# Dilated attention in a four-image transformer block: the sums over the taps move from VectorE to GpSimd

## The reference

```python
x = x + _L0_conv_ref(_ln_c(x), ...)        # halo attention
t = t + _L0_ffn_ref(_ln_t(t), ...)         # top-k routed feed-forward
x = x + _L1_conv_ref(_ln_c(x), ...)        # dilated attention, here is the change
t = t + _L1_ffn_ref(_ln_t(t), ...)         # graph attention routes a mixture of four experts

def _dilate_attention(q, k_, v, kernel, dil, head_dim):
    kw = _unfold_windows(k_, kernel, dil)   # nine shifted copies ("taps")
    vw = _unfold_windows(v, kernel, dil)
    attn = softmax(einsum('bndhw,bndkhw->bnkhw', qh, kw) * scale, axis=2)
    out = einsum('bnkhw,bndkhw->bndhw', attn, vw)      # the sum over nine taps
```

## Time and profile before

| what | value |
|---|---|
| median of 3 runs | 7053.45 us (7039.84 to 7058.35) |
| the profiled execution's own time | 7049.08 us |
| its span | 7047.3 us |
| mean granted TensorE clock | 0.693 of full speed |
| VectorE busy | 3414.0 us, 48% |
| TensorE busy | 2995.6 us, 43% |
| GpSimd busy | 2605.7 us, 37% |

### The profile page before, as it was taken

The page is one execution under the profiler, slowest core; times in us unless marked ns, Lnnn a source line. Parts: engine busy times, 40 slices in busy tenths (PEclk is TensorE's granted clock), DMA queues, the critical chain, the costliest instruction groups (busy, mean ns, idle before and its releaser), DMA issues.

```text
span 7047.3 us, 83154 instructions
## 1 busy us (share of the span) xinstructions
PE 2995.6 (43%) x31245; PEld 1791.3 (25%) x31245; DVE 3414.0 (48%) x7000; ACT 1543.3 (22%) x3959; POOL 2605.7 (37%) x2472
## 2 busy tenths in 40 slices
PE   0011149766987897788760222222222222222204
PEld 0011138424842673376220000000000000000103
DVE  9999988576857685777661111111111111111138
ACT  0000027403730463165200111111111111111100
POOL 0000000051011000100017777777777777777450
PEclk9975569866986798698755656565655555555556
DMA  2000040002000100010022222222122222222216
GB/s 82 0 0 0 0 168 4 4 18 56 4 12 1 40 3 1 13 17 3 1 33 22 34 33 33 33 33 33 28 31 33 33 29 31 33 33 33 65 46 218
DMA packets 259879, 227.73 MB, mean 32 GB/s; under 512 B 115180, under 2 KB 223128, under 8 KB 250456
## 3 DMA queue, kind: packets, MB, share of 16 engines
q0 software_dynamic: 78944, 29.28, 6.6%
q1 hardware_dynamic: 99960, 99.91, 4.6%
q10 hardware_dynamic: 80640, 93.86, 4.3%
HBM read 100.42 MB, written 121.39 MB: 31 GB/s over the span
## 4 chain that ended last, share of the span: by engine, by line
PE 27%; issue 20%; another core or an unknown queue 19%; DVE 19%; DVEq 7%; ACT 4%; DMA 3%; POOL 1%; ACTq 1%; SPq 0%
DVE SA_ L1325 3%; PE PSB L382 2%; PE PSB L1175 2%; DVE SA_ L1315 2%; PE PSB L686 2%; PE PSB L668 2%; PE PSB L352 2%; PE PSB L526 2%; DVEq L1406 2%; PE PSB L392 1%; PE PSB L518 1%; DVE SA_ L590 1%; DMA VPAD<-s_TNT 1%; PE PSB L366 1%
## 5 line engine op out<-in xcount | busy, mean ns | idle before, releaser
L962 POOL DMA_INDIRECT SA_<-s_T,GIX x2048 | 2166.4, 1058 | 675.7 <-issue 675.7
L1175 PE MATMUL PSB<-VPAD,EH 128*128 128x512 f32 x512 | 302.0, 754 | 1994.1 <-DMA VPAD<-s_TNT 1643.1
L907 DVE TENSOR_TENSOR XPAD<-SA_ 128x256 f32<-128x256 f32 x32 | 13.6, 425 | 1789.9 <-DMA SA_<-s_T,GIX 1789.9
L954 POOL DMA_INDIRECT s_AEXP<-fill,SIX x128 | 149.6, 1169 | 1557.3 <-DVE SA_ L587 1472.2
L858 POOL DMA_INDIRECT SA_<-s_SK,BLKI x128 | 131.5, 1028 | 1484.3 <-PE PSB L710 1389.0
L1175 PEld LDWEIGHTS PSB<-VPAD,EH 128*128 128x128 f32 x512 | 121.6, 246 | 2195.3 <-DMA VPAD<-s_TNT 1681.4
L1179 PE MATMUL PSB<-SA_,EW 128*128 128x512 f32 x512 | 345.6, 824 | 342.1 <-ACT SA_ L1160 181.0
L1429 PE MATMUL PSB<-ident,SA_ 128*128 128x128 f32 x448 | 83.1, 368 | 837.1 <-DVE SA_ L1396 575.1
L303 ACT ACTIVATE PRX<-PSB,MX 128x144 f32<-128x144 f32 x1024 | 375.2, 380 | 210.3 <-DVE MX L224 210.1
L1164 ACT ACTIVATE VPAD<-PSB,PRX 128x512 f32<-128x512 f32 x128 | 87.9, 687 | 1308.8 <-remote 969.0
L1160 ACT ACTIVATE SA_<-PSB,PRX 128x512 f32<-128x512 f32 x256 | 175.9, 687 | 770.6 <-issue 327.0
(11 more groups left out here) (365 smaller groups left out, 7339.3 us busy)
## 6 DMA issues: line engine op xcount, KB each, us to landing
SA_<-s_T,GIX POOLq DMA_INDIRECT x2048
s_Y<-VPAD ACTq DMA_DIRECT2D x32, 1024.0 KB
s_R<-zero SPq DMA_DIRECT2D x96, 256.0 KB, 2.9
s_R<-XPAD ACTq DMA_DIRECT2D x32, 768.0 KB
SB_<-s_Y SPq DMA_DIRECT2D x16, 1024.0 KB, 5.5
SA_<-s_Y SPq DMA_DIRECT2D x16, 1024.0 KB, 6.2
s_AEXP<-zero SPq DMA_DIRECT2D x32, 256.0 KB, 3.0
SA_<-in_x SPq DMA_DIRECT2D x16, 512.0 KB
```

The costliest lines, as they stand in the source:

```text
L962: pool.indirect_dma_start(out=n.G[:,s,c,:],out_offset=None,in_=d["T"],in_offset=IOA(ap=n.GIX[s][:,c:c+1],axis=0)).then_inc(n.gath[s],16)
L1175: pe.matmul(PSB[:,(m%4)*512:(m%4+1)*512],n.WM1[:,m//2,(m%2)*P:(m%2+1)*P],n.TNC[:,s,:],start=True,stop=True).then_inc(n.moe_h,1)
```

## The change

GpSimd does the additions over the taps. `value(m,j)` on VectorE keeps the multiplication alone. Its product goes to one of four buffers in turn: the two old ones, `REST`, and a piece of `SA`. Before it writes a buffer again it waits, on the new semaphore `s_ad`, for the addition four back. A new function `l1conv_pool` runs on GpSimd: for each unit and each tap j = 1 to 8 it waits for the product (`s_p2`), adds it to `ACC`, raises `s_ad`, possibly issues one indirect transfer, and drains. TensorE's `project` waits for `s_ad` in place of `s_acc`.

GpSimd's transfers are placed anew. Of the 128 block fetches, 48 are issued during image 0's feed-forward, 20 as keys and values are formed, and 60 behind the additions of image 0, one behind each. The 32 key fetches are unchanged. The scatters of images 1 to 3 come behind every second addition. The waits for `fill_done` and `np_rdy` stand before image 1's additions.

```diff
-    n.PRD=pr[:,0:6,:]; n.PR2=pr[:,6:8,:]; n.ACC=...
+    n.PRD=pr[:,0:6,:]; n.PR2=[pr[:,6,:],pr[:,7,:],n.REST[:,:],SA[:,19968:20480]]; n.ACC=...
@@ l1conv_dve
     def value(m,j):
         dve.wait_ge(n.s_ep,b*72+(9*m+j+1))
-        acc=n.ACC[:,m//2%2,m%2,:]; to=n.PR2[:,j%2,:] if j else acc
+        to=n.PR2[(j-1)%4] if j else n.ACC[:,m//2%2,m%2,:]
+        if j and 8*m+j>4: dve.wait_ge(n.s_ad,b*64+(8*m+j-4))
         bank=(9*m+j)%EBANKS
         dve.tensor_tensor(rows(to),rows(PSB[...]),tap(n.VD,m,TAPS[j]),ALU.mult).then_inc(n.s_p2,1)
-        if j:
-            dve.drain()
-            last=dve.tensor_tensor(acc,acc,to,ALU.add)
-            if j==8: last.then_inc(n.s_acc,1)
@@ l1conv_pe, project
-        if h==0: pe.wait_ge(n.s_acc,b*8+(2*u+2)); ...
+        if h==0: pe.wait_ge(n.s_ad,b*64+8*(2*u+2)); ...
@@ GpSimd
+HELD=48; PROJ=20
 def pos_pool(pool,m,n,d):
     pool.wait_ge(m.blk_rdy,1); pool.wait_ge(m.sk_st,16)
-    for t in range(NT):
-        if t<20: pool.wait_ge(n.s_kv,t+1)
-        else: pool.wait_ge(n.s_p2,(t-20)*66//108+1)
+    for t in range(HELD+PROJ):
+        if t<HELD: pool.wait_ge(n.s_h,t*2//3+1)
+        else: pool.wait_ge(n.s_kv,t-HELD+1)
+        block_pool(pool,m,n,d,t)
+def l1conv_pool(pool,m,n,d,b):
+    if b: pool.wait_ge(n.ad_ld,16*b)
+    for u in range(UNITS):
+        acc=n.ACC[:,u//2%2,u%2,:]
+        for j in range(1,9):
+            k=8*u+(j-1)
+            pool.wait_ge(n.s_p2,b*72+(9*u+j+1))
+            pool.tensor_tensor(acc,acc,n.PR2[(j-1)%4],ALU.add).then_inc(n.s_ad,1)
+            if b==0 and HELD+PROJ+k<NT: block_pool(pool,m,n,d,HELD+PROJ+k)
+            if b and j%2==0: start_pool(pool,n,d,(b-1)*TILES+k//2)
+            pool.drain()
@@ GpSimd's program
             pos_pool(pool,m,n,d)
+            l1conv_pool(pool,m,n,d,0)
+            keys_pool(pool,m,n,d)
+            pool.wait_ge(m.fill_done,FILLS); pool.wait_ge(n.np_rdy,1)
+            for b in range(1,IMGS): l1conv_pool(pool,m,n,d,b)
             V=blocks(pool,m)
-            pool.wait_ge(m.fill_done,FILLS)
             edges_pool(pool,n,d,m.tick,V)
```

More of the change, by code:

```diff
@@ L57, in declare_dense @@
     pr=SA[:,12288:16384].rearrange("p (k q) -> p k q",k=8)
-    n.PRD=pr[:,0:6,:]; n.PR2=pr[:,6:8,:]; n.ACC=SA[:,17408:19456].rearrange("p (u i q) -> p u i q",u=2,i=2)
+    n.PRD=pr[:,0:6,:]; n.PR2=[pr[:,6,:],pr[:,7,:],n.REST[:,:],SA[:,19968:20480]]; n.ACC=SA[:,17408:19456].rearrange("p (u i q) -> p u i q",u=2,i=2)
     n.LMX=sb("LMX",[P,4,8])
@@ L70, in declare_dense @@
     n.s_gt, n.s_tb, n.x3_st, n.tn_st, n.t_st, n.sorted_ = [sem(s) for s in ("s_gt", "s_tb", "x3_st", "tn_st", "t_st", "sorted_",)]
-    n.s_acc, n.s_ltc, n.s_lt, n.s_res = [sem(s) for s in ("s_acc", "s_ltc", "s_lt", "s_res",)]
+    n.s_ad, n.s_ltc, n.s_lt, n.s_res = [sem(s) for s in ("s_ad", "s_ltc", "s_lt", "s_res",)]
     n.s_ka, n.s_kd, n.s_p, n.s_pe, n.s_c0, n.s_r, n.s_c1, n.s_z = [sem(s) for s in ("s_ka", "s_kd", "s_p", "s_pe", "s_c0", "s_r", "s_c1", "s_z",)]
@@ L693, in project @@
         bank=pbank(u,h)
-        if h==0: pe.wait_ge(n.s_acc,b*8+(2*u+2)); pe.wait_ge(n.s_cqc,b*8+min(2*u+5,8))
+        if h==0: pe.wait_ge(n.s_ad,b*64+8*(2*u+2)); pe.wait_ge(n.s_cqc,b*8+min(2*u+5,8))
         if h==1 and u<3: pe.wait_ge(n.s_res,b*8+(2*u+1))
@@ L850, in pos_dve, with block_pool, keys_pool @@
     dve.drain()
+HELD=48; PROJ=20
+def block_pool(pool,m,n,d,t):
+    pool.indirect_dma_start(out=m.SI[:,t*BLK:(t+1)*BLK],out_offset=None,in_=d["SK"],in_offset=IOA(ap=m.BLKI[:,t:t+1],axis=0)).then_inc(n.gb_ld,16)
 def pos_pool(pool,m,n,d):
-    I=m.SI
     pool.wait_ge(m.blk_rdy,1); pool.wait_ge(m.sk_st,16)
-    for t in range(NT):
-        if t<20: pool.wait_ge(n.s_kv,t+1)
-        else: pool.wait_ge(n.s_p2,(t-20)*66//108+1)
-        pool.indirect_dma_start(out=I[:,t*BLK:(t+1)*BLK],out_offset=None,in_=d["SK"],in_offset=IOA(ap=m.BLKI[:,t:t+1],axis=0)).then_inc(n.gb_ld,16)
+    for t in range(HELD+PROJ):
+        if t<HELD: pool.wait_ge(n.s_h,t*2//3+1)
+        else: pool.wait_ge(n.s_kv,t-HELD+1)
+        block_pool(pool,m,n,d,t)
+def keys_pool(pool,m,n,d):
     pool.wait_ge(n.end_rdy,1)
@@ L862, in pos_pool, with start_pool @@
         if t>=4: pool.wait_ge(n.s_h,32+t-3)
-        pool.indirect_dma_start(out=I[:,t*128:(t+1)*128],out_offset=None,in_=rows,in_offset=IOA(ap=m.QI[:,t:t+1],axis=0)).then_inc(n.a2_ld,16)
+        pool.indirect_dma_start(out=m.SI[:,t*128:(t+1)*128],out_offset=None,in_=rows,in_offset=IOA(ap=m.QI[:,t:t+1],axis=0)).then_inc(n.a2_ld,16)
+def start_pool(pool,n,d,t):
+    pool.indirect_dma_start(out=d["AEXP"],out_offset=IOA(ap=n.SIX[:,t:t+1],axis=0),in_=n.ADN[:,t,:],in_offset=None,bounds_check=4096*128-1,oob_is_err=False).then_inc(n.ad_sc,16)
+def l1conv_pool(pool,m,n,d,b):
[9 more added lines that the diff above has]
+            pool.drain()
 def edges_prep_dve(dve,n,SA,V,ones,K,row):
@@ L945, in edges_pool @@
 def edges_pool(pool,n,d,tick,V):
[L947 to L954, removed]
+    pool.wait_ge(n.ad_ld2,16)
+    for t in range((IMGS-1)*TILES,NT): start_pool(pool,n,d,t)
     pool.wait_ge(n.d0_rdy,1)
```

## The result

| | before | after |
|---|---|---|
| median | 7048.5 us (7039.8 to 7058.4, 4 runs) | 7106.7 us (7106.0 to 7109.8, 4 runs) |
| span of the profiled execution | 7047.3 us | 7107.9 us |
| ratio | | 1.0083, 95% interval 1.0065 to 1.0100 |

The account below looks back on a forecast made before the run. The prediction took the bound to be a chain changing hands between VectorE and TensorE, neither full. Its terms summed to -81 + 30 + 22 + 8 = -21 us on 7049.1, giving 7028, stated as 7030; eight-in-ten range 6985 to 7085.

Parts of the forecast that it names:

- A transfer step: GpSimd's indirect fetch or scatter behind an addition: 0.94 us plus a 0.30 us gap, 1.25 us in all.
- rival 3: GpSimd becomes the bound, at image 0's buffer waits and all tails: 7060 us, near 7100 beyond the upper end; chance 0.20.
- The price of one addition: One addition on GpSimd: 1.15 us, middle of 0.69 and 1.57, plus a 0.30 us gap, 1.45 a step.
- Term 4: Image 0's units, where GpSimd's work nearly fills the unit: 2 us less gain in each of four units, 8 us.
- Term 3: Each image's tail, unit 7, where the projection waits for the slower GpSimd additions: 5.5 us lost an image, 22 in all.
- term 1: Additions leaving VectorE's chain in the four images: 26 x 0.78 = 20.3 us gained an image, 81 in all.
- term 2: GpSimd additions delaying VectorE's products and scaling at the same SBUF: 7.6 us lost an image, 30 in all.
- rival 2: Products and scaling wait in full for GpSimd additions: 14 us an image, 56 in all, total near 7050; chance 0.20.
- It just fits: Buffer wait within a unit: fourth addition ends about 2157.9 us, before the last multiplication is due at 2158.2, so no cost.
- Rival 1: GpSimd and VectorE do not disturb each other at SBUF, that cost is zero: total 6998 us; chance 0.18.
- Edits at nothing: 48 fetches moved to image 0's feed-forward, the moved waits and TensorE's clock were all counted as costing nothing.
- What would show it: Signs listed for right or wrong, such as additions of about 1.15 us and four stages together about 986 us, from 1007.

Follow-up runs that it names:

- the quarter additions: Changed kernel with each GpSimd addition covering only 128 of 512 columns, the other sums left out; 6990.0 us, 0.9929 of the kernel before.
- the fills: Changed kernel with each GpSimd addition replaced by a memset of 1024 columns of an unused tile, sums left out; 7030.5 us, 0.9978 of the kernel before.

## Why the prediction was wrong

The step that failed is "A transfer step is 0.94 + 0.30 = 1.25". I had read the 0.30 off two fetches in a row, with no drain behind either. With the drain a fetch costs 3.97 - 1.43 = 2.54 us and a scatter 5.16 - 2 x 1.43 = 2.30, twice as much. Image 0's unit was to hold 21.6 us of GpSimd and holds 31.8. That is the mechanism of rival 3, at its place, the wait on `s_ad` in image 0 and the tails. But I had tied it to an addition of 1.57 us or more and gave image 0's unit 25 us even then. The addition was not what was wrong.

Image 0's units were to be 20.3 - 7.6 - 8 = 4.7 us shorter and are 43.9 longer. These 49 us, 14 more in image 0's tail, 10.5 in the feed-forward, which I had put at nothing, and 8.5 in the tails of images 1 to 3 are the miss of about 80 us.

Point by point:

- *The price of one addition.* Forecast 1.15 + 0.30 = 1.45 a step, measured 1.26 + 0.17 = 1.43. That the sum is right is luck: the addition was too short and the gap too long by about the same. The estimate from the Trainium skill (GPSIMD Engine Reference, 3.1 Elementwise), 1.11 to 1.12 us, is 11% under the measured one.
- *Term 4, image 0: +8 us beside a gain of 20.* Measured 43.9 us longer units. With the drain ahead of the fetch 39 of these 44 us go, which shows the cause. With image 0 back on VectorE the whole loss of that image is gone.
- *Term 3, the tail: +5.5 an image.* Measured 8.1 to 8.6, and 19.6 in image 0. In images 1 to 3 three scatters at 2.30 instead of 1.25 add 3.2 us to the sum, which then gives 4.9 + 3.2 = 8.1. The same mis-sized step again. In image 0 four fetches at 2.54 make 6.1 + 5.2 = 11.3 of the 19.6. The other 8 are arrears: GpSimd begins unit 7's first addition at 1674.9 us, 9 us after its product was there, because it is still at work on unit 6.
- *Terms 1 and 2 in images 1 to 3: 20.3 - 7.6 = 12.7 us an image.* Measured 13.3 on average, and that the two agree so well is luck, because part of it is the clock, which I had counted as unchanged. Image 1's units had 440 matmuls in both kernels, before and after (columns as above, clock third last):

```profile
2116.80:2298.00 181.20, 133.33 (x440) 43.95 (x440) 138.36 (x243) 14.97 (x27) 30.52 (x28) 0.63 0.01 1
```

```profile
2195.00:2356.60 161.60, 119.91 (x440) 40.45 (x440) 112.34 (x187) 14.97 (x27) 102.11 (x81) 0.69 0.01 1
```

  TensorE does the same work in 120 us instead of 133. Six passes through the untouched units of images 1 to 3, in the kernel before and in the one with moved fetches, lie in order of their clock, from 180.9 us at 0.63 to 167.6 at 0.72. Here are two of them at 0.69 and 0.72, then the quarter additions and the fills at about the same clocks:

```profile
2140.30:2312.70 172.40, 126.22 (x440) 46.65 (x440) 137.67 (x242) 14.98 (x27) 30.53 (x28) 0.69 0.01 1
2784.60:2952.20 167.60, 122.91 (x440) 44.73 (x440) 137.66 (x243) 14.98 (x27) 30.34 (x28) 0.72 0.01 1
```

```profile
3407.60:3558.50 150.90, 121.63 (x440) 42.29 (x440) 103.39 (x186) 14.99 (x27) 59.61 (x84) 0.69 0.01 1
```

```profile
3445.00:3591.40 146.40, 113.90 (x440) 41.06 (x440) 100.40 (x186) 14.99 (x27) 80.30 (x83) 0.73 0.01 1
```

  At 0.69 to 0.70 untouched code takes 172.4 and 168.9 us, and full additions on GpSimd 159.2 to 163.2 in five passes, about 9 less. The quarter additions take 150.9, 20 less than untouched code, and the fills at 0.71 and 0.73 take 150.2 and 146.4, 19 less than 167.6. So my estimate at equal clock is a gross gain of 19 to 20 us, as term 1 had it, and a price of the full additions of about 10 to 11, more than term 2's 7.6 and less than rival 2's 14. Two or three us of this are scatter between passes. The price is not collisions alone: about 6 us an image are waits for a buffer, which the prediction had at nothing ("It just fits"). The products and the scaling have grown by 39.0 + 3.9 = 43 us in three images, 14 an image, but not all of that is on the chain. Rival 1 is excluded, since products and scaling are stretched. No run fixes the clock, so whether the change itself raises it is not shown.
- *Edits at nothing: the 48 fetches in the feed-forward.* +10.5 us in the change and +13.5 in the run that moves nothing else. "GpSimd was idle" was true and not the question: what the fetches cost there, others pay.
- *What would show it.* In most units of images 1 to 3 the fifth multiplication waits for its expansion, and the additions are 1.26 us long, as said. The four stages take 1054 us, not 986. A stage outside them did move, which I had named as a sign of being wrong. The sign I named for rival 3, multiplications that wait for GpSimd inside a unit, was the one that came: 92 us in image 0's units.

Open is why transfers in a row stop the other engines. The stalls carry no releaser, and on VectorE they last from 8 to 36 us, up to four in a stretch. I have nothing that tells apart a shared port, a shared queue and the supply of instructions. The DMA view has one hint: in the halo attention of image 2 before (2382 to 2643 us) it counts 49 packets of kind "instruction" on queue 8, and in the longest stall of the kernel with all transfers in a row (3123 to 3165 us) none. Whether they came late or were not asked for is not shown. Also not tried is GpSimd without any drain between dependent additions.

## What to carry to other kernels

When work moves to an engine that also issues transfers, price the pair in the order in which it will stand, with its drain, and not each by a row where it stands alone; and put the moved work where that engine's whole step, transfers included, is well under the step of the engine that it relieves. Leave the last unit of a stage on the faster engine, since nothing hides a slower one there. Two engines that read the same memory can pay for each other, here GpSimd's additions and VectorE's instructions with both inputs in SBUF: in images 1 to 3, a faster GpSimd queue made the kernel slower, and the pause behind its transfers made it faster.

## What was not expected of the hardware

- A drain on GpSimd behind an indirect transfer holds the engine for 1.3 us (scatter) to 1.6 us (fetch). Ahead of the transfer, behind an addition, the next transfer starts 0.9 us later, and the addition after the transfer at once.
- 48 block fetches during the feed-forward cost 10.5 to 13.5 us and 108 cost 87; 32 scatters in a row in a halo attention cost about 34 us. Between multiplications, in the kernel before, the same transfers cost little: taking 48 of them away from image 0's units changed these by 0.6 us, in single executions that can differ by more.
- A GpSimd addition stretched two VectorE products from 1.29 to up to 3.77 us. A GpSimd fill of 0.95 us stretched them by nothing.
- The same 440 matmuls and the same VectorE code took 180.9 us at a granted clock of 0.63 and 167.6 at 0.72. Stage times of single executions are comparable only beside their clocks.
